# A fused cross-attention and feed-forward block: the second feed-forward product, too, by Strassen's seven products

## The reference

```python
def xattn(x, ctx):
    q, k, v = x @ Wq + bq, ctx @ Wk + bk, ctx @ Wv + bv
    attn = softmax(clip(q @ k.T * scale, -CLAMP, CLAMP))
    return (attn @ v) @ Wo + bo
def ffn(x):
    hidden = x @ W1 + b1
    imag = w_imag * sin(theta + hidden * 0.1)
    q = hidden + (cos(theta) * w_real + sin(theta) * w_imag) * imag * 0.1
    return relu(q) @ W2 + b2
x = x + xattn(layernorm(x), ctx)
x = x + ffn(layernorm(x))
```

## Time and profile before

| | |
|---|---|
| Median of 3 runs | 1974.53 us (1973.66 to 1975.38) |
| Profiled execution | span 1974.9 us |
| TensorE (PE) busy | 1953.4 us, 99% |
| VectorE (DVE) busy | 1542.5 us, 78% |
| ScalarE (ACT) busy | 1262.7 us, 64% |
| GpSimd (POOL) busy | 517.0 us, 26%, nearly all before 804 us |
| HBM | 347.90 MB read, 91.23 MB written |

### The profile page before, as it was taken

The page is one execution under the profiler, slowest core; times in us unless marked ns, Lnnn a source line. Parts: engine busy times, 40 slices in busy tenths (PEclk is TensorE's granted clock), DMA queues, the critical chain, the costliest instruction groups (busy, mean ns, idle before and its releaser), DMA issues.

```text
span 1974.9 us, 27897 instructions
## 1 busy us (share of the span) xinstructions
PE 1953.4 (99%) x9162; PEld 1620.3 (82%) x9162; DVE 1542.5 (78%) x2360; ACT 1262.7 (64%) x2132; POOL 517.0 (26%) x365
## 2 busy tenths in 40 slices
PE   9999999999999999999999999999999999999999
PEld 7788888888887788777888888788788888878887
DVE  8988888888876986888588768868858876886773
ACT  6767767767754876667367557647746755764762
POOL 6877777777774321000000000000000000000000
PEclk9999999999999999999999999999999999999999
DMA  7455565565545999778778878877977887786745
GB/s 239 147 164 158 160 165 146 163 173 150 156 111 161 333 351 298 255 224 256 277 236 246 263 257 249 256 268 236 260 282 233 244 261 258 241 262 221 236 150 192
DMA packets 347459, 441.29 MB, mean 223 GB/s; under 512 B 165552, under 2 KB 201392, under 8 KB 347312
## 3 DMA queue, kind: packets, MB, share of 16 engines
q1 hardware_dynamic: 346448, 439.44, 71.3%
q10 hardware_dynamic: 864, 0.04, 0.0%
HBM read 347.90 MB, written 91.23 MB: 222 GB/s over the span
## 4 chain that ended last, share of the span: by engine, by line
PE 76%; DVE 11%; ACT 6%; issue 4%; POOL 2%; DMA 1%; SPq 0%; DVEq 0%; ACTq 0%; POOLq 0%
PE psum L1985 25%; PE psum L1987 24%; PE psum L1986 24%; PE psum L2078 3%; DVE frac L1789 1%; ACT turns L1363 1%; DVE stats L1472 1%; ACT x_sb L1163 1%; ACT frac L1339 1%; DVE act_lo L1810 1%; DVE temps L1515 1%; DVE hid L1803 1%; DVE x_sb L1827 1%; ACT act_hi L1391 1%; DVE late_hid L1784 1%
## 5 line engine op out<-in xcount | busy, mean ns | idle before, releaser
L1985 PE MATMUL psum<-w_ring,act_hi 128*128 128x512 f32 x1024 | 400.3, 391 | 2.0 <-DVE act_lo L1810 1.4
L1987 PE MATMUL psum<-w_ring,act_lo 128*128 128x512 f32 x1024 | 398.6, 389 | 0.0
L1986 PE MATMUL psum<-w_ring,act_hi 128*128 128x512 f32 x1024 | 398.4, 389 | 0.0
L1985 PE MATMUL psum<-xo,w_ring 128*128 128x512 f32 x784 | 308.4, 393 | 5.5 <-ACT p_sb L1346 4.5
L1986 PE MATMUL psum<-xo,w_ring 128*128 128x512 f32 x784 | 305.9, 390 | 0.0
L1987 PE MATMUL psum<-xo,w_ring 128*128 128x512 f32 x784 | 305.9, 390 | 0.0
L886 POOL TENSOR_TENSOR rstd<-var_eps,minus_half 128x4 f32<-128x4 f32 x32 | 38.6, 1207 | 948.9 <-DVE var_eps L1479 944.1
L1985 PEld LDWEIGHTS psum<-w_ring,act_hi 128*128 128x128 f32 x1024 | 192.2, 188 | 49.2 <-issue 10.1
L1789 DVE SCALAR_TENSOR_TENSOR frac<-frac,turns 128x512 f32<-128x512 f32 x256 | 173.7, 690 | 74.5 <-ACT frac L1339 74.5
L1376 ACT ACTIVATE frac<-frac 128x512 f32<-128x512 f32 x256 | 156.6, 627 | 109.6 <-DVE frac L1789 109.6
L1987 PEld LDWEIGHTS psum<-w_ring,act_lo 128*128 128x128 f32 x1024 | 192.2, 188 | 40.3
(11 more groups left out here) (188 smaller groups left out, 4291.4 us busy)
## 6 DMA issues: line engine op xcount, KB each, us to landing
w_ring<-w2s SPq DMA_DIRECT2D x240, 512.0 KB, 3.7
w_ring<-w1s SPq DMA_DIRECT2D x392, 256.0 KB, 3.6
x_sb<-turn_dram SPq DMA_DIRECT2D x58, 512.0 KB, 6.2
res<-in_x SPq DMA_DIRECT2D x64, 256.0 KB, 3.7
x_dram<-res SPq DMA_DIRECT2D x64, 256.0 KB, 3.0
acc<-x_dram SPq DMA_DIRECT2D x16, 1024.0 KB, 7.1
x_sb<-in_x SPq DMA_DIRECT2D x15, 1024.0 KB, 6.1
x_sb<-x_dram SPq DMA_DIRECT2D x15, 1024.0 KB, 7.4
```

Source lines behind the costliest of these rows:

```text
L1985: pe.matmul(o, a_hi, b_hi, start=first, stop=False, skip_group_check=resumed)
L1986: pe.matmul(o, a_hi, b_lo, start=False, stop=False, skip_group_check=resumed)
L1987: return pe.matmul(o, a_lo, b_hi, start=False, stop=last, skip_group_check=resumed)
```

## The change

The second product of each pair becomes a Strassen product as well. Its 2x2 blocks are two tiles by two chunks of hidden channels, and by the two halves of the 512 output channels. Steps and second product are no longer woven together: the eight steps of the first product come first, then 56 "parts" of the second (`OUT_PARTS`: seven products by eight pairs of chunks), each of 12 matmuls of 256 columns (`out_part`, in place of `second`).

- The four hidden quarters of a step lie side by side in `hidden4`, so `turn`, `whole`, `fraction`, `sine` and `wave` work on two quarters (1024 elements) at once, half as often.
- The ReLU of a whole pair of quarters goes to GpSimd (`positive`, 16 a pair, in place). Four kinds of sums of quarters that Strassen needs are formed on GpSimd as well, in place (`part_sum`, 16 a pair, 1024 elements each). `operand_sum`, the two bias adds of the next rows and those of the output rows move from VectorE to GpSimd.
- ScalarE rounds (`part_hi`) and VectorE subtracts (`part_lo`) 56 operands a pair, where there were 32. The ring of four stays.
- VectorE adds the seven products to the output rows in eight instructions a pair (`add_product`).
- PSUM: the steps alternate between banks 0 to 3 and 4 to 7, since the steps' banks are no longer shared with the second product.
- The plain pair forms four sums of W2 for each of eight pairs of chunks too (GpSimd 32 more sums of 128x256, ScalarE and VectorE 16 more splits), and stores them to DRAM (8 stores of 1 MB, 8 loads of 512 KB more). All weights now pass through `w1_ring`. P1, P2 and P3 of the second product read plain W2 in runs of 1 KB.

The diff, cut to its core:

```diff
-PRODUCTS = ("P1", "P6", "P4", "P2", "P5", "P7", "P3")
+HALF_C = C // 2
+
+PRODUCTS = ("P1", "P6", "P5", "P7", "P4", "P2", "P3")
...
+OUT_BANK = {"P2": 0, "P4": 2, "P1": 4, "P6": 4, "P7": 4, "P5": 6, "P3": 6}
+OUT_OPENS = ("P2", "P4", "P1", "P5")
+QUARTER_OF = {"P1": 0, "P7": 0, "P5": 1, "P2": 2, "P3": 2, "P4": 3, "P6": 3}
+OUT_PARTS = [("P2", 0), ("P2", 1)] + [part for p in range(FC // 4 * 2 - 2) for part in (("P1", p), ("P2", p + 2))] + \
+    [("P1", FC // 2 - 2), ("P1", FC // 2 - 1)] + [(name, p) for name in ("P4", "P5", "P6", "P3", "P7") for p in range(FC // 2)]
+NOUT = len(OUT_PARTS)
+OUT_AT = {part: k for k, part in enumerate(OUT_PARTS)}
+ADDED = (("P2", 0, 0, 1), ("P1", 0, 0, 1), ("P4", 1, 0, -1), ("P5", 1, 1, 1), ("P6", 0, 1, 1), ("P3", 0, 1, 1),
+         ("P7", 1, 0, 1), ("P7", 1, 1, 1))
+ADDED_AT = {20: 0, 22: 1, 26: 2, 33: 3, 41: 4, 49: 5}
...
+PART_SUMS = [(name, g) for g in range(FC // 4) for name in ("S3", "S1")] + [("S2", g) for g in range(FC // 4)] + \
+    [("S4", g) for g in range(FC // 4)]
+OPERAND_FROM = {"P5": "S1", "P6": "S2", "P3": "S4", "P7": "S3"}
...
+AHEAD = 4
...
-        turns = sbuf(pb, "turns", [P, 2, TOK])
-        frac = sbuf(pb, "frac", [P, 2, TOK])
-        hid = sbuf(pb, "hid", [P, 2, TOK])
+        turns = sbuf(pb, "turns", [P, 2, 2 * TOK])
+        frac = sbuf(pb, "frac", [P, 2, 2 * TOK])
         act_hi = sbuf(pb, "act_hi", [P, ACTS, TOK], F32R)
...
+        hidden4 = sbuf(pb, "hidden4", [P, FP, 4, TOK])
...
+                    name, p = OUT_PARTS[r - NP * FP]
+                    if name in W2_SUM_OF:
+                        source = w2x[p, W2_SUMS.index(W2_SUM_OF[name])]
+                        to = to.rearrange("p s x -> p (s x)")
+                    else:
+                        f, c = W2_PLAIN_OF[name]
+                        source = w2s[2 * p + f].rearrange("p (s c x) -> p s c x", s=2, c=2)[:, :, c]
+                sp.dma_start(to, source).then_inc(w1_in[n % W1_SLOTS], 16)
...
+            def positive(i, odd):
+                pool.wait_ge(wave_done, chain_at(i, odd) + 1)
+                rows = pair_rows(i % FP, odd)
+                pool.tensor_scalar(rows, rows, BIG, 0.0, ALU.min, ALU.max).then_inc(relu_done, 1)
...
+            def part_sum(T, name, g):
+
+                first, second, to, op = {"S3": (0, 1, 0, ALU.subtract), "S1": (1, 3, 1, ALU.add),
+                                         "S2": (3, 0, 3, ALU.subtract), "S4": (2, 3, 2, ALU.subtract)}[name]
+                if name == "S3":
+                    pool.wait_ge(relu_done, relu_at((T - 1) * FP + 2 * g + 1, 0))
+                    pool.wait_ge(act_lo_done, operand_at(T, OUT_AT["P1", 2 * g + 1]) + 1)
+                elif name == "S1":
+                    pool.wait_ge(s_done, sum_at(T, "S3", g))
+                elif name == "S2":
+                    pool.wait_ge(s_done, sum_at(T, "S1", g))
+                    pool.wait_ge(act_lo_done, operand_at(T, OUT_AT["P4", 2 * g + 1]) + 1)
+                else:
+                    pool.wait_ge(s_done, sum_at(T, "S2", g))
+                    pool.wait_ge(act_lo_done, operand_at(T, OUT_AT["P2", 2 * g + 1]) + 1)
+                quarters = [hidden4[:, 2 * g:2 * g + 2, q, :] for q in (to, first, second)]
+                pool.tensor_tensor(*quarters, op).then_inc(s_done, 1)
+
+            for T in range(1, FFN_PAIRS):
...
+            for T in range(1, FFN_PAIRS):
+                more = T + 1 < FFN_PAIRS
+                for p in range(FP):
+                    i = (T - 1) * FP + p
+                    if p >= 2:
+                        positive(i - 2, 0)
+                    if p >= 1:
+                        positive(i - 1, 1)
+                    if more and p in (3, 4):
+                        add_pair_rows(2 * T + 2, p - 3)
+                    if more and p in (5, 6):
+                        add_pair_rows(2 * T + 3, p - 5)
+                positive(i - 1, 0)
+                for name in ("S3", "S1"):
+                    part_sum(T, name, 0)
+                positive(i, 1)
+                positive(i, 0)
+                if more:
+                    rsqrt(TILES + 2 * T + 2)
+                for g in (1, 2):
+                    for name in ("S3", "S1"):
+                        part_sum(T, name, g)
+                if more:
+                    rsqrt(TILES + 2 * T + 3)
+                for name in ("S3", "S1"):
+                    part_sum(T, name, 3)
+                for s in range(2):
+                    for half in range(2):
+                        add_pair_acc(T, s, half)
+                for g in range(FP // 2):
+                    part_sum(T, "S2", g)
+                if more:
+                    operand_sum(T + 1, "T1")
+                    operand_sum(T + 1, "T2")
+                for g in range(FP // 2):
+                    part_sum(T, "S4", g)
+                if more:
+                    operand_sum(T + 1, "T4")
+                    operand_sum(T + 1, "T3")
 
             with pool.If_ne(count, P):
                 for s in range(2):
                     pool.wait_ge(out_stored[s], 16 * (FFN_PAIRS - s))
-                pool.wait_ge(last_stored, 16 * NB)
...
+            def part_hi(T, k):
+
+                (name, p), e = OUT_PARTS[k], operand_at(T, k)
+                if name in OPERAND_FROM:
+                    act.wait_ge(s_done, sum_at(T, OPERAND_FROM[name], p // 2))
                 else:
-                    act.wait_ge(wave_done, chain_at((T - 1) * FP + (r - FC) // 2, 3 - r % 2) + 1)
-                    source = late_hid[:, r - FC, :]
-                act.activation(act_hi[:, e % ACTS, :], source, ACT.Relu).then_inc(act_hi_done, 1)
+                    act.wait_ge(relu_done, relu_at((T - 1) * FP + p, int(name != "P1")))
+                if k >= ACTS:
+                    act.wait_ge(prod, at_out(T, k - ACTS))
+                elif T > 1:
+                    act.wait_ge(prod, at_out(T - 1, NOUT - ACTS + k))
...
-                        wave(chain_at(i - 1, 2))
+                    if p >= 2:
+                        wave(chain_at(i - 2, 0))
+                    if 4 <= p:
+                        part_lo(T, p - 4)
...
+                for k in range(NOUT - AHEAD):
+                    part_lo(T, k + AHEAD)
+                    if k == 0:
+                        fraction(chain_at(i, 1))
+                        fraction(chain_at(i, 0))
+                    if k == 1:
+                        wave(chain_at(i, 1))
+                    if k == 3:
+                        wave(chain_at(i, 0))
+                    if more and k in (5, 6):
+                        layer_stats(TILES + 2 * T + 2, half_blocks(k - 5))
+                    if more and k == 9:
...
+            def part_lo(T, k):
+                (name, p), e = OUT_PARTS[k], operand_at(T, k)
+                dve.wait_ge(act_hi_done, e + 1)
+                dve.tensor_tensor(act_lo[:, e % ACTS, :], hidden4[:, p, QUARTER_OF[name], :],
+                                  act_hi[:, e % ACTS, :].bitcast(F32), ALU.subtract).then_inc(act_lo_done, 1)
...
+                w, slot = w1_ring[:, n % W1_SLOTS], e % ACTS
+                for blk in range(NB):
+                    toks, cols = slice(blk * P, (blk + 1) * P), slice(blk % 2 * HALF_C, (blk % 2 + 1) * HALF_C)
+                    opens = p == 0 and blk % 2 == 0 and name in OUT_OPENS
+                    m = product(psum[:, OUT_BANK[name] + blk // 2, cols], (act_hi[:, slot, toks], act_lo[:, slot, toks]),
+                                (w[:, 0, :], w[:, 1, :]), opens, True, not opens)
```

More of the change, by code:

```diff
@@ L1112, in _ @@
             pool.memset(ones[:], 1.0).then_inc(last_done, 1)
-            for j in range(FC + HALF1):
+            for j in range(FC + HALF1 + 2):
                 pool.wait_ge(turns_done, j + 1)
@@ L1934, in _ @@
-                    if more and p in (3, 5):
-                        layer_shift(TILES + 2 * T + 2 + p // 5)
-                    fraction(chain_at(i, 0))
+                        fraction(chain_at(i - 1, 1))
+                        fraction(chain_at(i - 1, 0))
                     sum_v(i)
+                    hidden_22(i)
                     hidden_21(i)
-                    hidden_22(i)
-                    wave(chain_at(i, 0))
-                    if p == (0 if T > 1 else 2):
-                        for half in range(2):
-                            add_last_bias(2 * T, half)
@@ L1954, in _ @@
-                    wave(chain_at(i, 1))
-                    if more and p == 0:
-                        for half in range(2):
-                            add_row_bias(2 * T + 2, half)
-                    if more and p in (2, 3):
-                        add_row_bias(2 * T + 3, p - 2)
-                    if p in (5, 7):
-                        add_last_bias(2 * T + 1, p // 6)
-                hidden_12(i)
-                positive_lo(first_half(T, FC - 1))
-                wave(chain_at(i, 2))
@@ L1980, in _ @@
+                if more:
+                    add_product(T, 6)
```

(5 more changed lines are left out.)

574 lines of the change are left out of this document (341 added, 233 removed).

## The result

The changed kernel takes 2264.68 us (median of 4 runs, 2262.76 to 2267.50) against 1974.63 us (4 runs, 1973.66 to 1975.38) of the kernel before: 1.147 times as long, interval 1.145 to 1.149. The forecast was 2220, range 2040 to 2290.

A forecast was written before the change was run, and what follows sets the result against it. TensorE was taken to bound the kernel before. 804.4 + 10 + 5.4 + 6·(89.3 + 113) + (80.2 + 105) + 3.4 = 2222 us, stated as 2220, range 2040 to 2290.

The forecast's parts named there:

- TensorE bounds the kernel: In the seven pairs: TensorE's second product takes 80.0 us for 87.0, so 49 us at most are gained without waits.
- The small edit: Weight loads in the pairs: 256 KB land 3.6 us after issue, eight ring slots are 11 us ahead, so no cost.
- GpSimd and VectorE exclude each other: In the pairs: VectorE's two-SBUF-input instructions and GpSimd's reading ones wait for each other; VectorE's cost GpSimd 0.44 or 0.98 us.
- The ReLU at 1.5 us: GpSimd's ReLU of 1024 elements, priced midway between 1.22 and 1.907 us; 16 a pair make 24 us.
- First product 89.3 us: A pair's eight first-product steps take 89.3 us for 76.2, and 80.2 in the last pair.
- the same timetable: First product, one step in turns of VectorE and GpSimd: 12.7 us with row bias and remainder, 9.5 for TensorE alone.
- Second product 113 us: A pair's 56 second-product parts take 113 us for TensorE's 80.0, and 105 in the last pair.
- Plain pair +10, at most +24: The plain pair's extra sums, splits and 12.6 MB of transfers: between 0 and 24 us, taken as 10.
- Sum: Whole kernel: plain pair, left-over chunks, seven pairs and the end add up to 2222 us, stated as 2220.
- (a): Rival for the whole kernel: TensorE still sets the pace, VectorE's waits fall into its slack; 1929 us, chance 0.12.
- (b): Rival in the pairs: much of GpSimd's work hides in VectorE's gaps, about 167 us a pair; 1960 to 2000, chance 0.05.
- (c): Rival in the second product: weights of P1, P2, P3 in 1 KB runs come late, adding 10 to 30 us; chance 0.03.

The follow-up runs named there:

- thin: The changed kernel with all 44 GpSimd instructions of a pair on 8 elements instead of 1024, every wait kept: 1987.4 us.
- writes: The changed kernel with all 44 GpSimd instructions of a pair replaced by memsets of about the same length, which read nothing: 1998.17 us.

## Why the prediction was right

The direction, the mechanism and the place were right; three terms were off by 20 us and more, and partly cancelled. One reading was loose: the 166.7 us of a pair hold a share of the left-over chunks' 5.4 us, so a pair took 166.0.

- **TensorE bounds the kernel; the gain is 49 us at most.** Right as a ceiling. Without GpSimd's work 23 us came; 20 of the missing 26 are waits for weights. The small edit "256 KB land 3.6 us after issue, eight slots are 11 us ahead: nothing" was wrong by 20 us in the thin kernel; in the changed one TensorE's list of waits has none for weights, as it is behind VectorE.
- **GpSimd and VectorE exclude each other.** Shown four ways: by the means above, by `writes` (no reads, 266 us less), and by the kernel before with reads (299 us) and with writes (0.7 us). The Trainium skill ("SBUF — State Buffer", Who interferes with whom) says that a GpSimd instruction that only writes does not contend with a VectorE one of two SBUF inputs; these two runs agree.
- **The ReLU at 1.5 us.** Mis-sized: 1.04 at its shortest, 1.23 in the mean with its own waits. The Trainium skill ("GPSIMD Engine Reference", Engine selection) had one-input work at about line rate, and the trace agrees: 1.04 for 1024 elements, below the 1.24 of VectorE's one-input transpose of that size.
- **First product 89.3 us.** 83.8. Two things were off. The full steps are 11.5 us apart, not 12.7; with 1.05 for each of the two ReLUs the same timetable gives 11.8. And the steps without a row bias lose nothing: the third and fourth take 9.5 us where 9.8 and 12.0 were forecast, and the last pair's eight take 76.2 where 80.2 was. The row biases fell into steps 5 to 8, not 4 to 7. The first pair's product took 93.8, as its first two steps are 10 us longer in every version. Over the seven pairs (with the left-over chunks) 595 us for 621, 27 too many.
- **Second product 113 us.** 119.4 to 121.5, the last 107.7 for 105; together 828 for 783, 45 too few. In the pair from 1139.6 the last S2 is done after 63 us (58), T1 begins after 68 (67), T3 ends after 92 (89); the remainder after that takes 28 us, where 17 free parts were to take 24. The forecast had no term for the lower granted clock (0.94 here) in its sum, only 25 us without a working in its upper bound.
- **Plain pair +10, at most +24.** Failed: +30.7, outside its bounds. I looked at volumes (bytes, busy time) and not at the order in SyncE's list, which the diff showed: the lead of a load was cut from four blocks to one. Issuing them earlier gave 16 us; 4 to 5 are the transfers at most, and some 10 are open.
- **Sum.** 2222 + 20.7 (plain pair) - 27 + 45 + 2 (end) = 2263 us against a span of 2262.7. That 2220 was within 2% owes something to the cancelling.
- **Rivals.** (a) is out: TensorE waits for VectorE 221 us of the pairs' time (177.6 + 43.9). (b) is out as well, though the loss is less than GpSimd's whole time: 44 instructions of 83 us bare (28·2.365 + 16·1.04) cost 41.3. (c) is out: the parts from plain rows of 1 KB wait for no DMA in the changed kernel's list of waits, nor in that of `thin`, where TensorE waits for the stored sums (`w2x`) alone.

## What to carry to other kernels

An engine that is 2% busy is free only if nothing that bounds the kernel needs what it reads through. Beside a VectorE that is 75 to 80% busy with two-input work, GpSimd's reads cost about half of their own length in the end time here (41.3 of 83 us a pair, and 1.34 of 2.42 us). Where they stand counts: the same ReLUs cost nothing in the steps where they fell beside a sum out of PSUM or into a gap of VectorE (9.52 us a step in the last pair), and the added reads just ahead of the fraction cost most. Writes alone cost 0.7 us in the kernel before and 10.8 in the changed one. When a change doubles the stages of a pipeline, count for every load how many blocks lie between its issue and its use, before and after: a cut lead shows neither in bytes nor in busy shares.
